# Turning the tokens of three half-stages on VectorE with small DMAs instead of on TensorE

## The reference

```
x = x + tanh(g_xattn) * cross_attention(layernorm(x), ctx)      # 16 heads of 128, q and k rms-normed
x = x + tanh(g_ffn)   * decoder_layer(layernorm(x))             # below

def decoder_layer(y):
    h = rmsnorm(y) * ln1_w
    y = y + causal_attention(h) @ wo                            # 16 heads of 128
    t = rmsnorm(y) * ln2_w
    return y + routed_experts(t, top 6 of 16) + shared_expert(t)
```

## Time and profile before

| | |
|---|---|
| median of 3 runs | 629.57 us (629.23 to 630.35) |
| the profiled execution's own time | 628.85 us |
| its span, from the first to the last instruction | 627.1 us |
| granted TensorE clock | 1.000 of full speed |
| busy share of the span | PE 99%, DVE 74%, ACT 51%, POOL 40% |
| DMA | 50.30 MB, 80 GB/s on the mean |

### The profile page before, as it was taken

How to read it: one execution, slowest core, us unless ns; L and a number is a source line. 1 busy time by engine, 2 the same in 40 slices (tenths; PEclk the granted TensorE clock), 3 DMA queues, 4 the chain that set the end, 5 groups by cost and what they waited for, 6 DMA issues and landing times.

```text
span 627.1 us, 18234 instructions
## 1 busy us (share of the span) xinstructions
PE 619.1 (99%) x7200; PEld 541.5 (86%) x7200; DVE 462.0 (74%) x930; ACT 320.5 (51%) x699; POOL 253.3 (40%) x336
## 2 busy tenths in 40 slices
PE   8999999999999999999999999999999999999997
PEld 6788888888889988999999889988888888888886
DVE  5979777997886886786677899565576987555556
ACT  6867677777743334242434333453477444444442
POOL 3221211313144334344343354345545665455453
PEclk9999999999999999999999999999999999999999
DMA  7532131111021322222231321123323233333332
GB/s 234 186 85 70 52 103 28 40 40 31 24 70 43 111 69 69 70 68 77 64 118 39 115 70 36 35 63 93 98 85 94 75 102 101 90 87 99 100 87 90
DMA packets 36023, 50.30 MB, mean 80 GB/s; under 512 B 4080, under 2 KB 23024, under 8 KB 35952
## 3 DMA queue, kind: packets, MB, share of 16 engines
q1 hardware_dynamic: 35376, 48.81, 26.2%
q10 hardware_dynamic: 576, 0.48, 0.2%
HBM read 48.22 MB, written 1.05 MB: 79 GB/s over the span
## 4 chain that ended last, share of the span: by engine, by line
PE 96%; DVE 1%; ACT 1%; DMA 1%; issue 1%; SPq 0%; DVEq 0%; ACTq 0%
PE acc L568 26%; PE bank_q L541 17%; PE bank_k L541 14%; PE bank_v L541 9%; PE bank_s L541 8%; PE bank_v L656 7%; PE bank_k L736 2%; PE bank_p L753 2%; PE bank_s L714 2%; PE bank_s L704 2%; PE bank_t L721 1%; PE bank_p L687 1%; PE bank_q L677 1%; PE bank_k L666 1%; DMA xt<-in_ctx_t 1%
## 5 line engine op out<-in xcount | busy, mean ns | idle before, releaser
L568 PE MATMUL acc<-wo_hi,pv_hi 128*128 128x256 f32 x328 | 93.4, 285 | 0.4 <-DVE pv_lo L1515 0.2
L568 PE MATMUL acc<-wo_lo,pv_hi 128*128 128x256 f32 x328 | 92.9, 283 | 0.0
L568 PE MATMUL acc<-wo_hi,pv_lo 128*128 128x256 f32 x328 | 92.0, 281 | 0.0
L1677 POOL TENSOR_TENSOR wq_lo<-raw_a,wq_hi 128x256 fp32r<-128x256 f32 x32 | 23.4, 732 | 116.9 <-DVE wq_hi L1452 116.9
L568 PEld LDWEIGHTS acc<-wo_hi,pv_hi 128*128 128x128 f32 x328 | 61.5, 188 | 5.3 <-issue 2.2
L1677 POOL TENSOR_TENSOR wq_lo<-raw_m,wq_hi 128x256 fp32r<-128x256 f32 x50 | 40.4, 808 | 59.8 <-DVE wq_hi L1471 58.3
L568 PEld LDWEIGHTS acc<-wo_lo,pv_hi 128*128 128x128 f32 x328 | 61.6, 188 | 2.2
L568 PEld LDWEIGHTS acc<-wo_hi,pv_lo 128*128 128x128 f32 x328 | 62.3, 190 | 0.0
L1515 DVE TENSOR_TENSOR pv_lo<-raw_a,pv_hi 128x512 fp32r<-128x512 f32 (+1 forms) x51 | 37.5, 737 | 31.8 <-ACT pv_hi L1104 31.5
L1104 ACT ACTIVATE pv_hi<-raw_a 128x512 fp32r<-128x512 f32 (+1 forms) x51 | 31.7, 623 | 56.1 <-DVE raw_a L1510 50.5
L541 PE MATMUL bank_q<-xt_hi,wq_hi 128*128 128x512 f32 x144 | 59.8, 415 | 0.0
(11 more groups left out here) (246 smaller groups left out, 1949.2 us busy)
## 6 DMA issues: line engine op xcount, KB each, us to landing
raw_m<-in_chunk_m SPq DMA_DIRECT2D x50, 256.0 KB, 2.8
raw_a<-in_head_a SPq DMA_DIRECT2D x48, 192.0 KB, 3.3
raw_b<-in_head_b SPq DMA_DIRECT2D x32, 256.0 KB, 3.0
raw_m<-in_chunk_m SPq DMA_DIRECT2D x50, 128.0 KB, 2.1
raw_v<-in_pair_v SPq DMA_DIRECT2D x16, 256.0 KB, 2.8
raw_b<-in_head_b SPq DMA_DIRECT2D x32, 128.0 KB, 2.1
xs<-in_x SPq DMA_DIRECT2D x6, 128.0 KB, 3.2
out<-xs SPq DMA_DIRECT2D x3, 256.0 KB, 2.5
```

The source lines that it names most:

```text
L568: last = nc.tensor.matmul(acc[t // 2][:, (t % 2) * D:(t % 2 + 1) * D], w[:, tok], m, start=begins and n == 0, stop=True, skip_group_check= ...
L1677: nc.gpsimd.tensor_tensor(lo, raw, hi, ALU.subtract).then_inc(signal, 1)
```

## The change

The half-stages x1, y0 and y1 no longer turn their tokens on TensorE. x0, t0 and t1 still do.

- **blocks** (DVE): two 128 x 512 stream transposes turn `hn` within blocks of 32 x 32 into a new tile `blocks`.
- **moves** (SP): 16 DMAs within SBUF carry the blocks to the partitions where they belong, into `xt` (`turned_x`). Each takes 32 partitions to 32 others, 8 runs of 32 floats (128 B) from each partition: 256 runs, 32 KB. For x1 they are issued in two groups of 8, for y0 and y1 in one group of 16. SP waits first until the blocks are ready.
- **split**: ACT waits for all 16, then rounds `xt` to `xt_hi` (two 128 x 512), and POOL, no longer DVE, makes `xt_lo` (two 128 x 512).
- Places: x1 has `stats`, `norm`, `blocks`, `split` beside pairs 1, 2, 3, 6 of a0 (before: `stats`, `norm`, `turn` beside 3, 4, 5). y0 and y1 have `blocks` beside pair 5 and `split` beside pair 6.
- The weight `ln1_w` is applied in `scale`, along the features, so `scale` is a scalar_tensor_tensor with two SBUF inputs; `ln1_w` is loaded as 256 columns of every partition, by the second load of the small tensor.
- With no turn in the a and b0 stages, `key_sums` always lies in `bank_p`, and a wait of TensorE for `xt_lo` before the context product is gone.

```
-    beside_pairs("a", 0, ("x", 1), stats=(pairs - 5, 2), norm=(pairs - 4, 2), turn=(pairs - 3, 0))
+    beside_pairs("a", 0, ("x", 1), stats=(pairs - 7, 2), norm=(pairs - 6, 2), blocks=(pairs - 5, 0),
+                 split=(pairs - 2, 0))
     beside_pairs("a", 1, ("y", 0), stats=(1, 2), rough=(1, 1), norm=(2, 2), sums=(3, 0), root=(3, 1), scale=(4, 2),
-                 turn=(5, 0))
+                 blocks=(5, 0), split=(6, 0))
...
+            def move_blocks(step, to=range(QUADS)):
+                sp.wait_ge(blocks_ready, MOVED[step])
+                sp.wait_ge(ctxt_lo_ready, HALVES)
+                sp.wait_ge(xt_lo_ready, KD * PREP[step])
+                for m in to:
+                    found = blocks[:].rearrange("p (b m r) -> p b m r", m=QUADS, r=GROUP)[:, :, m, :]
+                    place = turned_x[m * GROUP:(m + 1) * GROUP].rearrange("c (b a r) -> c b a r", a=QUADS, r=GROUP)
+                    for a in range(QUADS):
+                        sp.dma_start(place[:, :, a, :], found[a * GROUP:(a + 1) * GROUP]).then_inc(ld_blocks, 16)
...
                 if n + 2 < HALVES * PAIRS:
                     reload_a1(n + 2)
+                if n in (4, 5):
+                    move_blocks(("x", 1), range(2 * n - 8, 2 * n - 6))
+                if n == PAIRS + 6:
+                    move_blocks(("y", 0))
...
                 if n + 1 < HALVES * PAIRS:
                     reload_b1(n + 1)
+                if n == 6:
+                    move_blocks(("y", 1))
                 for h in range(2):
                     sp.wait_ge(B["wo_lo"], numbered("b", n - 1).of(h))
                     load_b2(numbered("b", n), h)
...
+                if piece == "split":
+                    act_e.wait_ge(ld_blocks, 16 * QUADS * QUADS * MOVED[step])
+                    for k in range(KD):
+                        nc.scalar.activation(by_chunk(xt_hi[step[1]][:, k, :]), chunk_of(k), ACT.Copy).then_inc(xt_hi_ready, 1)
...
+                            dve.mark(nc.vector.scalar_tensor_tensor(hn[:, t, :], ys[:, half, t, :], st[:, 2, t:t + 1], weights,
+                                                                    ALU.mult, ALU.mult))
...
+                if piece == "blocks":
+                    v.wait_ge(dve.sem, dve.n)
...
+                    for t in range(0, NT, 2):
+                        last = nc.vector.transpose(blocks[:, t * D:(t + 2) * D], hn[:, t:t + 2, :].rearrange("p t d -> p (t d)"))
+                    last.then_inc(blocks_ready, 1)
...
+                if piece == "split":
+                    for k in range(KD):
+                        pool.wait_ge(xt_hi_ready, KD * PREP[step] + k + 1)
+                        rest(by_chunk(xt_lo[step[1]][:, k, :]), chunk_of(k), by_chunk(xt_hi[step[1]][:, k, :]), xt_lo_ready)
...
                 for h in range(2):
                     split_head(after, h)
+                    if not h:
+                        prepare(u)
```

More of the change, by code:

```diff
@@ L177, in beside_pairs @@
             pieces[kind, half, i, slot] = (name, step)
-    beside_pairs("a", 0, ("x", 1), stats=(pairs - 5, 2), norm=(pairs - 4, 2), turn=(pairs - 3, 0))
+    beside_pairs("a", 0, ("x", 1), stats=(pairs - 7, 2), norm=(pairs - 6, 2), blocks=(pairs - 5, 0),
+                 split=(pairs - 2, 0))
     beside_pairs("a", 1, ("y", 0), stats=(1, 2), rough=(1, 1), norm=(2, 2), sums=(3, 0), root=(3, 1), scale=(4, 2),
-                 turn=(5, 0))
-    beside_pairs("b", 0, ("y", 1), stats=(1, 1), norm=(2, 1), sums=(3, 0), root=(3, 1), scale=(4, 1), turn=(5, 0))
+                 blocks=(5, 0), split=(6, 0))
+    beside_pairs("b", 0, ("y", 1), stats=(1, 1), norm=(2, 1), sums=(3, 0), root=(3, 1), scale=(4, 1), blocks=(5, 0),
+                 split=(6, 0))
     beside_pairs("b", 1, ("t", 0), sums=(0, 1), root=(1, 0), scale=(1, 1), turn=(2, 0), logits=(3, 0), equals=(3, 1),
@@ L224, in flamingo_layer @@
     M1, M2 = 2 * D, D
-    SM_GQ, SM_GK, SM_LN1, SM_LN2, SM_GX, SM_GF, SM_GATE = 0, 1, 2, 4, 6, 7, 8
+    SM_GQ, SM_GK, SM_LN2, SM_GX, SM_GF, SM_GATE = 0, 1, 2, 4, 5, 6
     SM_ID = SM_GATE + KD * E
@@ L229, in flamingo_layer @@
     SM_TIE = SM_MASK + SEQ
-    SM_W = SM_TIE + E * E
+    SM_LNROW = SM_TIE + E * E
+    SM_W = SM_LNROW + D
     with ExitStack() as stack:
@@ L254, in flamingo_layer @@
         hn = sb("hn", [P, NT, D])
+        blocks = sb("blocks", [P, NT * D])
+        turned_x = xt[:].rearrange("p k n -> p (k n)")
         ones, ones_of = sb("ones", [P, 1]), sb("ones_of", [P, SEQ])
@@ L345, in flamingo_layer @@
         pe_cw = sem("pe_cw")
+        blocks_ready, ld_blocks = sem("blocks_ready"), sem("ld_blocks")
         tok_ready, first_tokens = sem("tok_ready"), sem("first_tokens")
@@ L375, in flamingo_layer, with chunk_of, by_chunk @@
         PREP = {(step, half): n for n, (step, half) in enumerate((s_, h_) for s_ in "xyt" for h_ in range(HALVES))}
+        MOVED = {("x", 1): 1, ("y", 0): 2, ("y", 1): 3}
+        TURNED = {("x", 0): 0, ("t", 0): 1, ("t", 1): 2}
         piece_at, run_units = plan.piece, plan.run
+        def chunk_of(k):
+            return turned_x.rearrange("p (t k n) -> p t k n", k=KD, n=P)[:, :, k, :]
+        def by_chunk(ap):
+            return ap.rearrange("p (t n) -> p t n", n=P)
         def turn_banks(u):
-            return (bank_t, bank_p) if u.kind == "a" else (bank_p, bank_s if u.kind == "b" else bank_t)
+            return bank_p, bank_s if u.kind == "b" else bank_t
         def query_bank(u, h):
@@ L405, in key_sums @@
         def key_sums(u):
-            turned = u.n > 1 and plan.piece(u.prev())[0] == "turn"
-            return (bank_v if turned else bank_p)[:, 0:HT // 2]
+            return bank_p[:, 0:HT // 2]
         def gate_bank(u):
@@ L757, in turn_tokens @@
             def turn_tokens(step, banks):
-                pe.wait_ge(tok_ready, PREP[step])
+                pe.wait_ge(tok_ready, TURNED[step])
                 for k, bank in enumerate(banks):
@@ L794, in prepare @@
                 return []
-            def turned_tokens(u):
-                piece, step = piece_at(u)
-                return [(xt_lo_ready, KD * (PREP[step] + 1))] if piece == "turn" else []
             def release(held):
@@ L823, in cross_pair @@
                         pe.wait_ge(A["vo_lo"], prev.n)
-                    release(turned_tokens(prev))
                     context_values(prev)
@@ L967, in take_tokens @@
                 for k, bank in enumerate(banks):
-                    act_e.wait_ge(pe_tr, KD * PREP[step] + k + 1)
+                    act_e.wait_ge(pe_tr, KD * TURNED[step] + k + 1)
                     def take(target):
@@ L972, in take @@
                             return nc.scalar.activation(target[:, k, :], bank[:], ACT.Copy)
-                        col = (SM_LN1 if kind == "y" else SM_LN2) + k
+                        col = SM_LN2 + k
                         return nc.scalar.activation(target[:, k, :], bank[:], ACT.Identity, scale=sm[:, col:col + 1])
                     if kind == "t" and not half:
+                        act_e.wait_ge(xt_lo_ready, KD * PREP[step])
                         last = take(xt)
@@ L1282, in prepare_piece @@
                     if PREP[step]:
-                        v.wait_ge(pe_tr, KD * PREP[step])
+                        v.wait_ge(pe_tr, KD)
                     for t in range(NT):
@@ L1287, in prepare_piece @@
                             last.then_inc(first_tokens, 1)
-                    if PREP[step]:
-                        last.then_inc(tok_ready, 1)
+                        else:
+                            dve.mark(last)
                 if piece == "norm" and kind != "x":
@@ L1301, in prepare_piece @@
                 if piece in ("scale", "apply"):
-                    v.wait_ge(pe_tr, KD * PREP[step])
+                    if kind == "y":
+                        v.wait_ge(ld_rest, 16)
                     for t in range(NT):
-                        last = nc.vector.tensor_scalar(hn[:, t, :], ys[:, half, t, :], st[:, 2, t:t + 1], None, ALU.mult)
-                    last.then_inc(tok_ready, 1)
+                        if kind == "y":
+                            weights = sm[:, SM_LNROW:SM_LNROW + D]
+                            dve.mark(nc.vector.scalar_tensor_tensor(hn[:, t, :], ys[:, half, t, :], st[:, 2, t:t + 1], weights,
+                                                                    ALU.mult, ALU.mult))
+                        else:
+                            v.wait_ge(pe_tr, KD * TURNED[step])
+                            last = nc.vector.tensor_scalar(hn[:, t, :], ys[:, half, t, :], st[:, 2, t:t + 1], None, ALU.mult)
+                    if kind == "t":
+                        last.then_inc(tok_ready, 1)
+                if piece == "blocks":
+                    v.wait_ge(dve.sem, dve.n)
+                    if MOVED[step] > 1:
+                        v.wait_ge(ld_blocks, 16 * QUADS * QUADS * (MOVED[step] - 1))
+                    for t in range(0, NT, 2):
```

(10 more changed lines are left out.)

5 lines of the change are left out of this document (3 added, 2 removed).

## The result

The changed kernel takes **644.79 us** (median; 643.71 to 645.86) beside 629.64 for the kernel before on the same chip: a ratio of **1.0241, 95% interval 1.0226 to 1.0255**. The forecast of 631.4 had the sign but an eighth of the size (1.8 of 15.2 us), and the time lies outside the range. The profiled span is 641.7 us, 14.6 more than before; the mean granted clock 0.991.

A forecast was written before the change was run, and what follows sets the result against it. TensorE's program was taken to bound the kernel (PE 96% of the chain). Terms -2.6 (three turns removed) + 0.5 + 0.5 + 0.3 + 2.2 + 0.9 = +1.8 us gave 631.4 us on the median; range 626.9 to 637.0.

The forecast's parts named there:

- The statistics in pair 1 of a0: x1's statistics, two pairs earlier, exceed DVE's idle time in pair 1 of a0 and delay `sc_sub`: +0.5 us.
- `ssq` behind POOL: In a0, DVE's `ssq` waits for POOL's low-part subtractions and delays `sc_sub`: +0.5 us.
- Scale: Applying ln1_w in DVE's four scale instructions takes longer before pair 5 of a1: +0.3 us; hidden in b0.
- the first stall: Pair 6 of a1: y0's last move lands late, ACT's `qt` releases TensorE's `norm_k` late: +2.2 us.
- SP needs 0.47 us from issue to issue: SP's queue: step taken from loads and stores; y0's sixteenth issue comes 15 steps later, landing 2.0 us after issue.
- the second query projection behind `qt`: Pair 6 of b0: `load_v`, queued behind y1's moves, makes DVE's copy of queries late for this projection: +0.9 us.
- POOL's low parts of y0: In a1, costed at nothing because TensorE waits for something else; without that cover, another 0.5 us.
- ACT's `split` in pair 6 finds its data: In b0, y1's sixteen issues end at 274.2, so ACT's rounding need not wait for them: no cost.
- Short packets are costly: Rival, chance 0.2: 128 B runs in the moves cost up to 74 ns each; halfway case 635.2 us, decisive from 29 ns.
- Small things: Second load of the small tensor grows 128 KB, eight more packets per DMA engine, at most 0.6 us later: taken as 0.
- Nothing reaches TensorE: Rival, chance 0.1: no added delay, DVE's included, reaches TensorE; the whole -2.6 us is gained, 627.0 us.
- The moves land in time: Rival, chance 0.2: moves of y0 and y1 cost nothing, so -1.3 us, 628.3 us.

The follow-up runs named there:

- e_early_all: As e_early, plus x1's statistics, norm and blocks one pair later, its moves issued in groups of 4 and 12, POOL's low parts before its heads: 630.04 us, ratio 1.0017.
- e_runs: Against the changed kernel: same 48 moves of 32 KB within SBUF, each in 32 runs of 1 KB instead of 256 of 128 B: 643.91 us, ratio 1.0221.
- e_from_dram: Against the kernel with 32 runs of 1 KB per move: the 48 moves read rows of x in DRAM instead of blocks in SBUF: 635.35 us, ratio 1.0095.
- e_two_queues: Against the changed kernel: half of each half-stage's moves issued by GpSimd (POOL), the other half by SP: 631.58 us, ratio 1.0042.
- e_nomoves: Against the changed kernel: the 48 moves left out, ACT and POOL split the blocks as they lie: 630.86 us, ratio 1.0009.
- e_early: Against the changed kernel: blocks and moves of y0 and y1 placed earlier, in pair 4 of a1 and b0, all issued by SP: 631.19 us, ratio 1.0029.

## Why the prediction was wrong, step by step

**Right.** The three turns gave 0.87 each (a1.5: -0.37 with scale's 0.53 in it). The statistics in pair 1 of a0 cost 0.70 (0.5 predicted), `ssq` behind POOL 0.46 (0.5): e_early_all takes both away. Scale took 1.67 for 1.14, +0.53 (0.3). x1's moves delay nothing. The place and the releaser of the first stall were as predicted, and a move lands 2.0 us after its issue.

**The step that failed** is "SP needs 0.47 us from issue to issue", taken for moves within SBUF. That neither bytes nor runs show in it was right (e_runs); that a source in SBUF costs no more was wrong (e_from_dram), and no row of before had such a DMA. Nor did the sum have a term for single long issues. The trace had a bound on that side, a load of 1.37 us by SP among 32 in a0 and a1, but I gave the step no upper end at all. With 0.65, the steps of y0 are 15 x 0.18 = 2.7 longer and two long issues add 1.36: 4.1 us, and 2.2 + 4.1 = 6.3. TensorE stood for 5.92; that the pair's 6.34 agrees so closely is partly luck, since some 0.4 of it is `norm_k` at the lower clock. In b0 `load_v` was issued 13.4 us after the first move, not 8.5, so 4.9 later: 1.85 + 4.9 = 6.75 late at DVE (6.92 idle). TensorE met it one wait earlier than I had said, at `turn_attn` behind DVE's `attn`, not at the second query projection behind `qt`. So the mechanisms held in the main, and the sizes came from the time of SP's row of 16 issues.

**Missing terms.** First, the clock: TensorE stood for 5.5 us in b0 and the pair lost 7.27; of the 1.8 between them 0.2 is an "issue" pause and some 1.5 are matmuls at the lower level (0.70 granted over the 5 us behind the stall). In e_two_queues a stall of 1.3 us left the granted clock at 1.00. Second, POOL's low parts of y0, costed at nothing under the cover of another wait, cost 0.7 to 0.8 in a1.7 once that cover was taken away. The text had named 0.5 for that case, but for `ssq` beside POOL; what comes late is the low part itself, which the text had put ahead of TensorE only because TensorE would be delayed. Third, "ACT's `split` in pair 6 finds its data": ACT waited 2.38 for it, behind TensorE's longer wait. About 0.8 of the 14.6 lies in pauses of pairs that the table doesn't name.

**The rivals.** "Short packets are costly" fell: 13,056 more packets took (0.273 x 641.7 - 0.262 x 627.1) x 16 = 174 us, 13 ns each, under the 29 from which it decides; against e_nomoves (35,376 packets, 26.6% of 629.5 us) it is 9. The Trainium skill (DMA: Bandwidth & Descriptors, Bandwidth) says that copies within SBUF are spared the penalty of small descriptors. The trace agrees in so far as these packets stay under 29 ns. The eight more packets for each DMA engine under "Small things" aren't there: e_nomoves has the longer load of the small tensor and as many packets as before. "Nothing reaches TensorE" (627.0) fell with the 0.70 and the 0.46 in a0. "The moves land in time" (628.3) was wrong for this kernel, but e_early_all is that case, at 630.0: above it by blocks in a full pair of DVE (1.15) and by POOL beside DVE's casts (1.02), though a0's costs are gone from it.

## What to carry to other kernels

A constant that multiplies a long serial chain needs a row of the same kind (queue, source, destination) or a wide range of its own: 0.18 us on each issue and two long issues in each row became 14 us on the kernel. When many DMAs are put into an in-order queue, ask both when the last one lands and what is issued behind it; putting the loads first cured their stall here and made the moves late instead. When one wait covers another engine's work, price that work as if the wait were gone. Starting them sooner or sharing them between two queues took the stalls away here, while moving the waiting instruction only moved them. Of three turns two were worth replacing; the third had no free time on DVE and POOL to be replaced with.

## What the runs showed of the hardware

- SP needs 0.46 us from one issue to the next with a source in DRAM (e_from_dram) and 0.65 with a source in SBUF (the change; 0.63 in e_runs), for 32 KB into 32 partitions each; POOL's issues from SBUF last 0.58 (e_two_queues).
- In a row of 16 issues by SP two took 1.2 to 1.8 us, with either source, in y0 and y1 of the change, e_runs and e_from_dram; in e_early's row of y1 none took over 0.72, and on POOL the longest of 24 took 0.72.
- After TensorE had stood for 5.5 to 5.9 us, the granted clock was 0.64 and 0.87 in 5 us windows of matmuls behind it (the change); behind a stall of 1.3 us it was 1.00 (e_two_queues).
- Beside POOL's subtractions of 128x512 a DVE `ssq` of 128x8 took 0.68 (the change) and 0.77 (e_nomoves), in place of 0.17 in pair 6 of a0 before; a cast of 128x256 took 1.37 (e_early_all) in place of 0.28.
